# A transformer layer on eight cores: projection weights loaded in eight slices, and the residual load issued by GpSimd

## The chip, the cores and the metric

The kernel runs on all 8 cores of one Trainium2 chip. Each core computes one batch element of eight on its own; the cores exchange nothing. The metric is device time in microseconds of the slowest core. Each core has TensorE (PE, matrix products), VectorE (DVE), ScalarE (ACT), GpSimd (POOL), SyncE (SP) and 16 DMA engines. DMAs are issued here from SP's queue (SPq) and from POOL's queue (POOLq).

## What is computed

One layer of four sub-layers on `x` of shape (8, 2048, 1024), each with its residual. The same `ffn` sub-layer, which is an attention with mixture-of-experts low-rank terms in its projections, is used twice.

```python
x = L0_attn_a_x
x = x + attn_a(layernorm(x), ...)   # causal attention, 16 heads of 64         ("a1")
x = x + ffn(layernorm(x), ...)      # full attention, MoE low-rank projections ("f1")
x = x + attn_b(layernorm(x), ...)   # retention, below                         ("b1")
x = x + ffn(layernorm(x), ...)      # the same as f1                           ("f2")

# attn_b, cut:
q = (x @ Wq.T).reshape(B, L, H, DH)
v = (x @ Wv.T).reshape(B, L, H, DH)
state = _retention_scan(v, jax.nn.sigmoid(beta))
y = (q * state).reshape(B, L, D)
y = (y - mu) * jax.lax.rsqrt(var + LN_EPS) * ln_gamma + ln_beta
y = y * jax.nn.silu(x @ Wg.T)
return y @ Wo.T
```

## The kernel before

Activations are kept transposed: 1024 features in 8 tiles of 128 partitions (`ND = 8`), 2048 positions in 4 chunks of 512 (`NC = 4`, `CH = 512`). `XLN` is the normalised input, `ACT2` the input of an output projection; both are 8 tiles of 128x2048 in bf16. Weights lie in HBM as f32 and are cast to bf16 by the DMA, which for that reason is issued by POOL.

The kernel is a list of stages (`nc.Block`), each with one hand-written program per engine, ordered by semaphores. At the end of a block all engines meet, so no DMA of a stage is issued before the stage before has ended. Seven stages have the same inner form, a product of a 1024x1024 weight with 8 activation tiles:

- **The output projections**, `emit_oproj`, called for a1, f1, b1 and f2. The weight tile is `WOB` (128 x 8x1024, bf16). In a1, f1 and f2 (`do_cn`) the stage first normalises the attention's context: 512 small matmuls on PE and 64 multiplications on DVE. Then, in f1 and f2 (`ffn`), come 32 matmuls for the low-rank term. Then the projection, a loop over `dt2` (0 to 7, output tiles of 128 features), here called a **step**, with four chunks in each. A chunk is 8 accumulating matmuls of 128x128 by 128x512 (L1119), with a ninth in f1 and f2 (L1125), into one of **two** PSUM banks. DVE adds the old residual (`XOLD`) and writes `XNEW` (L1150 or L1155). PE may be two chunks ahead of DVE. SP stores `XNEW` to HBM (L1048); before that it has loaded `XOLD` (L1063), 128x2048 f32, 1 MB. Both tiles have two buffers. In a1, f1 and b1 the next LayerNorm's column sums (8 short matmuls, L152 and L157, for tile `dt2`-2) stand at the head of a step from step 2 on. f2 has none.
- **The Q, V and G projections of `attn_b`**, in `emit_attnb`, blocks `bq`, `bv` and `bg`. The weight tile is `WB`, chunks go into three PSUM banks, 8 matmuls each (L1231, L1309, L1471). In `bv` DVE scans along time after every step.

Before the change each weight comes in two DMAs of 512 columns (1024 KB of bf16 each), counted by the semaphores `gq` and `gqb`. PE waits for the first half ahead of step 0 and for the second ahead of step 4. In the output projection SP's order is: `XOLD` 0, `XOLD` 1, then for each later step: wait until DVE has finished step `dt2`-2, load `XOLD` `dt2`, store `XNEW` `dt2`-2.

The semaphore `to` (`tp`, `tv`, `tg2` in `attn_b`) counts chunks that PE has finished, `vo` chunks that DVE has finished, `oq` the loads of `XOLD`, `so` the stores.

Of the kernel before, what the change touches and what calls it, by code (L numbers as in the profile page):

```python
# [16 lines left out]
ND = 8  # L17
# [5 lines left out]
NC = 4  # L23
# [924 lines left out]
def emit_oproj(P, bufs, tag, wo_name, src_res_name, dst_name, ffn,  # L948
# [3 lines left out]
    src_res = bufs[src_res_name]  # L952
# [8 lines left out]
    with (nc.sbuf_tensor(f"wob{tag}", [128, ND * D], BF16)) as WOB, (  # L961
# [71 lines left out]

        @blk.gpsimd
        def _(g):
            for j, ctr in enumerate((gq, gqb)):
                ctr.inc(g.dma_start(
                    WOB[:].rearrange("p (t o) -> p t o", t=ND)[
                        :, :, j * 512:(j + 1) * 512],
                    bufs[wo_name][:, j * 512:(j + 1) * 512].rearrange(  # L1040
                        "(t p) o -> p t o", p=128)), 16)

        def _store(sync, dt2):
            sync.wait_ge(vo.sem, vo0 + nxvso_holder[0] + NC * (dt2 + 1))
# [5 lines left out]

        @blk.sync
        def _(sync):
            for nm in ("sto0", "sto1"):
                if P.ctr[nm].v > so0[0] + so0[1]:
                    pass
            sync.wait_ge(so[0].sem, so0[0])
            sync.wait_ge(so[1].sem, so0[1])
            for dt2 in range(ND):
                if dt2 >= 2:
                    sync.wait_ge(vo.sem, vo0 + nxvso_holder[0] +  # L1060
                                 NC * (dt2 - 1))
                oq[dt2 % 2].inc(
                    sync.dma_start(XOLD[dt2 % 2][:],  # L1063
                                   src_res[dt2 * 128:(dt2 + 1) * 128, :]), 16)
                if dt2 >= 2:
                    _store(sync, dt2 - 2)
            _store(sync, ND - 2)
            _store(sync, ND - 1)
            sync.wait_ge(so[0].sem, so0[0] + 16 * (ND // 2))
            sync.wait_ge(so[1].sem, so0[1] + 16 * (ND // 2))  # L1070

# [27 lines left out]

        @blk.tensor  # L1100
        def _(t):
            t.wait_ge(gq.sem, gq0 + 16)
            t.wait_ge(vn.sem, vn0 + ncn)
            if ffn:
                t.wait_ge(vo.sem, vo0 + NC)
            ng = 0
            for dt2 in range(ND):
                if dt2 == 4:
                    t.wait_ge(gqb.sem, gqb0 + 16)
                if ln is not None and dt2 >= 2:  # L1110
                    ln.colsums(t, dt2 - 2)
                for ch in range(NC):
                    ng += 1
                    if ng > 2:
                        t.wait_ge(vo.sem, vo0 + nxvso + ng - 2)
                    bank = (ng - 1) % 2
                    last = None
                    for dt in range(ND):
                        last = t.matmul(  # L1119
                            PSB[bank][:],  # L1120
                            WOB[:, dt * D + dt2 * 128:dt * D + (dt2 + 1) * 128],
                            ACT2[dt][:, ch * CH:(ch + 1) * CH],
                            start=(dt == 0), stop=((not ffn) and dt == ND - 1))
                    if ffn:
                        last = t.matmul(  # L1125
                            PSB[bank][:],
                            bufs["UP"]["o"][:, dt2 * 128:(dt2 + 1) * 128],
                            bufs["XVS"]["o"][:, ch * CH:(ch + 1) * CH],
                            start=False, stop=True)
                    to.inc(last)  # L1130
            if ln is not None:
                ln.colsums(t, ND - 2)
                ln.colsums(t, ND - 1)
# [47 lines left out]
def emit_attnb(P, bufs):  # L1181
# [4 lines left out]
    with ExitStack() as es:  # L1186
# [7 lines left out]
        gq0b = gqb.v  # L1194
        with (nc.sbuf_tensor("lamr", [1, 16], F32) as LAMR,
# [2 lines left out]

            @blk.gpsimd
            def _(g):  # L1200
                for j, ctr in enumerate((gq, gqb)):
                    ctr.inc(g.dma_start(
                        WB[:].rearrange("p (t o) -> p t o", t=ND)[
                            :, :, j * 512:(j + 1) * 512],
                        bufs["bWqT"][:, j * 512:(j + 1) * 512].rearrange(
                            "(t p) o -> p t o", p=128)), 16)

            @blk.sync
# [7 lines left out]

            @blk.tensor
            def _(t):
                t.wait_ge(gq.sem, gq0 + 16)
                ng = 0  # L1220
                for dt2 in range(ND):
                    if dt2 == 4:
                        t.wait_ge(gqb.sem, gq0b + 16)
                    for ch in range(NC):
                        ng += 1
                        if ng > 3:
                            t.wait_ge(vp2.sem, vp0 + ng - 3)
                        bank = (ng - 1) % 3
                        last = None
                        for dt in range(ND):  # L1230
                            last = t.matmul(  # L1231
                                PSB[bank][:],
                                WB[:, dt * D + dt2 * 128:dt * D + (dt2 + 1) * 128],
                                XLN[dt][:, ch * CH:(ch + 1) * CH],
                                start=(dt == 0), stop=(dt == ND - 1))
                        tp.inc(last)
# [45 lines left out]
        with (nc.sbuf_tensor("bvt", [128, T], BF16) as VB,  # L1282
              nc.sbuf_tensor("bscn", [128, T], F32) as SCN,
              nc.Block("bv") as blk):

            @blk.gpsimd
            def _(g):
                for j, ctr in enumerate((gq, gqb)):
                    ctr.inc(g.dma_start(
                        WB[:].rearrange("p (t o) -> p t o", t=ND)[  # L1290
                            :, :, j * 512:(j + 1) * 512],
                        bufs["bWvT"][:, j * 512:(j + 1) * 512].rearrange(
                            "(t p) o -> p t o", p=128)), 16)

            @blk.tensor
            def _(t):
                t.wait_ge(gq.sem, gq1 + 16)
                ng = 0
                for dt2 in range(ND):
                    if dt2 == 4:  # L1300
                        t.wait_ge(gqb.sem, gq1b + 16)
                    for ch in range(NC):
                        ng += 1
                        if ng > 3:
                            t.wait_ge(vv.sem, vv0 + (ng - 3) + (ng - 3) // 4 * 2)
                        bank = (ng - 1) % 3
                        last = None
                        for dt in range(ND):
                            last = t.matmul(  # L1309
                                PSB[bank][:],  # L1310
                                WB[:, dt * D + dt2 * 128:dt * D + (dt2 + 1) * 128],
                                XLN[dt][:, ch * CH:(ch + 1) * CH],
                                start=(dt == 0), stop=(dt == ND - 1))
                        tv.inc(last)

            @blk.vector
            def _(v):
                ng = 0
                for dt2 in range(ND):
                    v.wait_ge(vv.sem, vv.v)  # L1320
                    for ch in range(NC):
                        ng += 1
                        v.wait_ge(tv.sem, tv0 + ng)
                        bank = (ng - 1) % 3
                        vv.inc(v.tensor_copy(VB[:, ch * CH:(ch + 1) * CH],
                                             PSB[bank][:]))
                    v.wait_ge(vv.sem, vv.v)
                    vv.inc(v.tensor_tensor_scan(
                        SCN[:], LAMC[:, dt2:dt2 + 1].broadcast_to([128, T]),
                        VB[:], 0.0, ALU.mult, ALU.add))  # L1330
                    v.wait_ge(vv.sem, vv.v)
                    vv.inc(v.tensor_tensor(ACT2[dt2][:], QT[dt2][:], SCN[:],
                                           ALU.mult))
# [109 lines left out]
        with (nc.sbuf_tensor("bgt0", [128, T], BF16) as gt0,  # L1443
# [3 lines left out]

            @blk.gpsimd
            def _(g):
                for j, ctr in enumerate((gq, gqb)):  # L1450
                    ctr.inc(g.dma_start(
                        WB[:].rearrange("p (t o) -> p t o", t=ND)[
                            :, :, j * 512:(j + 1) * 512],
                        bufs["bWgT"][:, j * 512:(j + 1) * 512].rearrange(
                            "(t p) o -> p t o", p=128)), 16)

            @blk.tensor
            def _(t):
                t.wait_ge(gq.sem, gq2 + 16)
                ng = 0  # L1460
                for dt2 in range(ND):
                    if dt2 == 4:
                        t.wait_ge(gqb.sem, gq2b + 16)
                    for ch in range(NC):
                        ng += 1
                        if ng > 3:
# [262 lines left out]
```

## Time and profile before

| | us |
|---|---|
| median of 3 runs | 4083.34 |
| lowest and highest | 4075.66 and 4128.11 |
| the profiled execution | 4081.07 |
| its span on the slowest core (core 1) | 4079.5 |
| PE busy | 3068.7 (75%) |
| ACT busy | 1612.8 (40%) |
| DVE busy | 1317.8 (32%) |
| POOL busy | 71.2 (2%) |

The profile covers one execution, on the slowest core. Its page gives the busy time of the engines and the costliest groups of instructions; the trace behind it can be asked for single instructions, for windows of time, for waits, and for the DMAs with their time from issue to landing. The granted clock is TensorE's, as a share of 2.4 GHz. Names of tiles carry the stage: `wobf` is `WOB` in f1 and f2, `xoa`, `xof`, `xob` are `XOLD`, `xna`, `xnf`, `xnb` are `XNEW`, `bwb` is `WB`, `qsla` and `ksla` are 128-column slices of the Q and K weights in the attention of a1 (cast from f32 as well, 256 KB of bf16). The size beside a DMA is that of what is written.

### The profile page before, as it was taken

The page shows a single profiled execution, that of the slowest core. Times are in us where ns is not written, and L with a number is a line of the kernel's source. Part 1 is how long each engine was busy: PE and PEld are TensorE (multiplying, and loading weights), DVE is VectorE, ACT ScalarE, POOL GpSimd, SP SyncE. Part 2 cuts the span into 40 slices and gives each one's busy share as a digit, 9 for nine tenths or more (in the row PEclk, how much of TensorE's full clock was granted, in tenths as well). Part 3 has the DMA queues.
Part 4 walks back from the last instruction along what each step waited for, and adds up shares of the span by engine and source line. Part 5 has one row for each costly group of instructions (what it writes and reads, how often), then busy time and mean ns, then how long its engine had stood idle before and what let it go on. Part 6 is the DMA issues. An engine that isn't in the chain of part 4 may idle for free. (4 is left out here: it accounts for less than half of the span.)

```text
span 4079.5 us, 40781 instructions; the slowest of 8 cores (4055.3 to 4079.5 us)
## 1 busy us (share of the span) xinstructions
PE 3068.7 (75%) x13815; PEld 1267.1 (31%) x13815; DVE 1317.8 (32%) x1955; ACT 1612.8 (40%) x1600; POOL 71.2 (2%) x88
## 2 busy tenths in 40 slices
PE   2678788787557888888887756457387888888888
PEld 0223333334223333333324222122132333333334
DVE  4333333335452222112115445532622111121134
ACT  2034444452300566666672400134003666666640
POOL 0000000000000000000000000000000000000000
PEclk6887888879769888888889877678588888888889
DMA  2200010002321000000002411016211000000014
GB/s 94 31 6 6 6 11 6 1 1 64 122 42 21 6 6 6 6 6 6 1 1 42 145 21 21 0 26 181 31 21 16 6 6 6 6 6 1 1 42 145
DMA packets 95037, 119.22 MB, mean 29 GB/s; under 512 B 61785, under 2 KB 84458, under 8 KB 85500
## 3 DMA queue, kind: packets, MB, share of 16 engines
q0 software_dynamic: 80192, 37.75, 7.5%
q1 hardware_dynamic: 14652, 78.87, 6.1%
q8 instruction: 124, 2.03, 0.2%
q14 instruction: 69, 0.57, 0.0%
HBM read 120.81 MB, written 33.55 MB: 38 GB/s over the span
## 5 line engine op out<-in xcount | busy, mean ns | idle before, releaser
L794 ACT ACTIVATE ringf<-psd,negcb 128x1024 bf16<-128x1024 f32 x1024 | 1060.0, 1124 | 606.4 <-PE psd L742 605.7
L794 ACT ACTIVATE ringa<-psd,negcb 128x1024 bf16<-128x1024 f32 x320 | 337.4, 1116 | 362.5 <-PE psd L742 331.7
L722 PE MATMUL psb<-ringf,vprf 128*65 128x512 bf16 x1024 | 445.7, 435 | 10.4 <-ACT ringf L794 9.1
L739 PE MATMUL psd<-qpairf,kpairf 64*128 64x512 bf16 x1024 | 421.5, 424 | 28.7 <-ACT ringf L794 6.1
L742 PE MATMUL psd<-qpairf,kpairf 64*128 64x512 bf16 x1024 | 429.9, 432 | 0.0
L726 PE MATMUL psb<-ringf,vprf 128*65 128x512 bf16 x1024 | 422.6, 413 | 0.0
L696 PE MATMUL psb<-c_IDENT,densf 1*128 1x1 f32 x1024 | 171.6, 293 | 172.8 <-DVE act L896 172.8
L739 PEld LDWEIGHTS psd<-qpairf,kpairf 64*128 64x128 bf16 x1024 | 91.7, 95 | 459.3 <-issue 458.1
L696 PEld LDWEIGHTS psb<-c_IDENT,densf 1*128 1x128 f32 x1024 | 168.0, 252 | 190.3 <-issue 190.3
L722 PEld LDWEIGHTS psb<-ringf,vprf 128*65 128x65 bf16 x1024 | 114.2, 112 | 301.4 <-issue 293.7
L772 ACT ACT_TABLE_LOAD x3 | 3.8, 1283 | 495.6 <-DVE grow L847 495.6
L818 DVE TENSOR_SCALAR qpairf<-psb,fbq 128x512 bf16<-128x512 f32 x64 | 48.0, 751 | 372.2 <-PE psb L662 372.2
L722 PE MATMUL psb<-ringa,vpra 128*65 128x512 bf16 x320 | 138.4, 433 | 36.9 <-DVE ringa L873 36.3
L696 PE MATMUL psb<-c_IDENT,densa 1*128 1x1 f32 x512 | 101.0, 322 | 84.3 <-DVE act L896 84.3
L822 DVE TENSOR_SCALAR kpairf<-psb,fbk 128x512 bf16<-128x512 f32 x64 | 48.1, 751 | 342.8 <-PE psb L662 342.8
L656 PE MATMUL psb<-xln,qslf 128*128 128x512 bf16 x512 | 136.9, 416 | 23.1 <-DMA kslf<-fWkT 17.1
L552 PE MATMUL psd<-wvbf,xln 128*128 128x512 bf16 x512 | 128.3, 396 | 27.4 <-DMA wvbf<-fWvT 27.4
L888 DVE COPY densf<-psb 1x512 f32<-1x512 f32 x64 | 43.8, 685 | 301.1 <-PE psb L726 299.0
L1011 PE MATMUL psd<-c_IDENTB,reciph 128*64 128x128 bf16 x768 | 110.5, 225 | 39.8 <-DVE act L1029 29.3
L873 DVE TENSOR_TENSOR ringa<-ringa,c_MASKS 128x1024 bf16<-128x1024 bf16 x128 | 88.6, 692 | 150.6 <-ACT ringa L794 150.6
L739 PE MATMUL psd<-qpaira,kpaira 64*128 64x512 bf16 x320 | 134.5, 440 | 3.1 <-ACT ringa L794 0.9
L656 PE MATMUL psb<-xln,kslf 128*128 128x512 bf16 x512 | 130.2, 400 | 8.1 <-DVE kpairf L822 6.0
(273 smaller groups left out, 4040.7 us busy)
## 6 DMA issues: line engine op xcount, KB each, us to landing
xof<-Xs SPq DMA_DIRECT2D x16, 1024.0 KB, 7.3
lnsta<-xT SPq DMA_DIRECT2D x8, 1024.0 KB, 5.7
xoa<-xT SPq DMA_DIRECT2D x8, 1024.0 KB, 6.7
Xs<-xna SPq DMA_DIRECT2D x8, 1024.0 KB, 8.7
Xs<-xnf SPq DMA_DIRECT2D x8, 1024.0 KB, 10.3
xob<-Xs SPq DMA_DIRECT2D x8, 1024.0 KB, 6.7
Xs<-xnb SPq DMA_DIRECT2D x8, 1024.0 KB, 8.5
y<-xnf SPq DMA_DIRECT2D x8, 1024.0 KB, 8.6
```

Source lines behind the costliest of these rows:

```text
L552: last = t.matmul(PSB[bank][:], XLN[dt][:, m * 128:(m + 1) * 128], WVB[:, dt * 512:(dt + 1) * 512], start=(dt == 0), stop=((not ffn) and d ...
L656: last = t.matmul(PSB[bank][:], sl[p % 2][:, dt * 128:(dt + 1) * 128], XLN[dt][:, ch * CH:(ch + 1) * CH], start=(dt == 0), stop=((not ffn) ...
L696: last = t.matmul(DEN[:, col:col + 1], DENS[0:1, half * 2 * CH + h01 * CH + sub * 128: half * 2 * CH + h01 * CH + (sub + 1) * 128], bufs[" ...
L722: t.matmul(PSB[4][0:65, :], VP[tkpv][:, hA * 65:hA * 65 + 65], RING[slot][:, 0:512], start=(tkpv == 0), stop=(tkpv == n - 1))
L726: last = t.matmul(PSB[5][0:65, :], VP[tkpv][:, hB * 65:hB * 65 + 65], RING[slot][:, 512:1024], start=(tkpv == 0), stop=(tkpv == n - 1))
L739: t.matmul(pd[:, 0:512], KP[p % 2][0:64, ks], QP[p % 2][0:64, cs], start=True, stop=True, tile_position=(0, 0))
L742: ts.inc(t.matmul(pd[:, 512:1024], KP[p % 2][64:128, ks], QP[p % 2][64:128, cs], start=True, stop=True, tile_position=(64, 0)))
L794: ex.inc(s.activation(RING[slot][:], pd[:], AF.Exp, bias=NEGC[:, p:p + 1], scale=softmax_scale))
L818: ins = v.tensor_scalar(dstb[p % 2][:, cs], PSB[7][:], bufs["FBQ"][:, p:p + 1], ASCALE, ALU.add, ALU.mult)
L822: ins = v.tensor_scalar(dstb[p % 2][:, cs], PSB[7][:], bufs["FBK"][:, p:p + 1], None, ALU.add)
L873: vm.inc(v.tensor_mul(RING[slot][:], RING[slot][:], ms))
L1011: last = t.matmul(PSB[bank][0:64, sub * 128:(sub + 1) * 128], rp[:, col:col + 1].broadcast_to([128, 64]), bufs["IDENTB"][:], start=(rp is ...
```

## The change

- Each of the seven weights comes in eight DMAs of 128 columns (one for each step) in place of two of 512, alternately on `gq` and `gqb`. Slices 0 and 1 are issued at the start of the stage; slice j from 2 on is issued after PE has finished step j-2. PE waits for slice `dt2` at the head of step `dt2`.
- In the output projection the load of `XOLD` moves from SP's program to POOL's, between the weight slices. POOL's order is: slices 0 and 1, then for `dt2` from 0 to 7: wait until DVE has finished step `dt2`-2 (from `dt2` = 2), load `XOLD` `dt2`, and, up to `dt2` = 5, wait until PE has finished step `dt2` and load slice `dt2`+2.
- SP's program keeps the stores alone.

What is computed, and from what, stays the same. The core of the diff (the blocks `bv` and `bg` change as `bq` does):

```diff
         @blk.gpsimd
         def _(g):
-            for j, ctr in enumerate((gq, gqb)):
-                ctr.inc(g.dma_start(
+            def wob_dma(j):
+                (gq, gqb)[j % 2].inc(g.dma_start(
                     WOB[:].rearrange("p (t o) -> p t o", t=ND)[
-                        :, :, j * 512:(j + 1) * 512],
-                    bufs[wo_name][:, j * 512:(j + 1) * 512].rearrange(
+                        :, :, j * 128:(j + 1) * 128],
+                    bufs[wo_name][:, j * 128:(j + 1) * 128].rearrange(
                         "(t p) o -> p t o", p=128)), 16)
+
+            off = NC if ffn else 0
+            wob_dma(0)
+            wob_dma(1)
+            for dt2 in range(ND):
+                if dt2 >= 2:
+                    g.wait_ge(vo.sem, vo0 + nxvso_holder[0] + NC * (dt2 - 1))
+                oq[dt2 % 2].inc(
+                    g.dma_start(XOLD[dt2 % 2][:],
+                                src_res[dt2 * 128:(dt2 + 1) * 128, :]), 16)
+                j = dt2 + 2
+                if j < ND:
+                    g.wait_ge(to.sem, to0 + off + (j - 1) * NC)
+                    wob_dma(j)
...
             for dt2 in range(ND):
-                if dt2 >= 2:
-                    sync.wait_ge(vo.sem, vo0 + nxvso_holder[0] +
-                                 NC * (dt2 - 1))
-                oq[dt2 % 2].inc(
-                    sync.dma_start(XOLD[dt2 % 2][:],
-                                   src_res[dt2 * 128:(dt2 + 1) * 128, :]), 16)
-                if dt2 >= 2:
-                    _store(sync, dt2 - 2)
-            _store(sync, ND - 2)
-            _store(sync, ND - 1)
+                _store(sync, dt2)
...
         @blk.tensor
         def _(t):
-            t.wait_ge(gq.sem, gq0 + 16)
             t.wait_ge(vn.sem, vn0 + ncn)
...
             for dt2 in range(ND):
-                if dt2 == 4:
-                    t.wait_ge(gqb.sem, gqb0 + 16)
+                t.wait_ge((gq, gqb)[dt2 % 2].sem,
+                          (gq0, gqb0)[dt2 % 2] + 16 * (dt2 // 2 + 1))
...
             @blk.gpsimd
             def _(g):
-                for j, ctr in enumerate((gq, gqb)):
-                    ctr.inc(g.dma_start(
+                for j in range(ND):
+                    if j >= 2:
+                        g.wait_ge(tp.sem, tp0 + (j - 1) * NC)
+                    (gq, gqb)[j % 2].inc(g.dma_start(
                         WB[:].rearrange("p (t o) -> p t o", t=ND)[
-                            :, :, j * 512:(j + 1) * 512],
-                        bufs["bWqT"][:, j * 512:(j + 1) * 512].rearrange(
+                            :, :, j * 128:(j + 1) * 128],
+                        bufs["bWqT"][:, j * 128:(j + 1) * 128].rearrange(
                             "(t p) o -> p t o", p=128)), 16)
```

## Rows read from the trace of the kernel before

**Rows 1.** The page: its head, and PE's line of the engine table.
```profile
span 4079.5 us, 40781 instructions; the slowest of 8 cores (4055.3 to 4079.5 us)
...
PE 3068.7 (75%) x13815; PEld 1267.1 (31%) x13815; DVE 1317.8 (32%) x1955; ACT 1612.8 (40%) x1600; POOL 71.2 (2%) x88
```

**Rows 2.** Windows: output projections (a1, f1, wait before b1, b1, f2); Q; V; G.
```profile
core 1: us, PE busy (x) PEld busy (x) DVE busy (x) ACT busy (x) POOL busy (x), PEclk, DMA share, GB/s
1002.60:1064.60 62.00, 61.98 (x306) 26.33 (x308) 21.46 (x32) 27.25 (x15) 0.00 (x0) 1.00 0.71 221
2237.40:2307.80 70.40, 69.25 (x340) 29.48 (x342) 23.41 (x32) 27.26 (x15) 0.00 (x0) 1.00 0.62 194
2750.20:2766.00 15.80, 0.00 (x0) 0.00 (x0) 0.00 (x0) 0.00 (x0) 1.75 (x2) 0.55 0.93 210
2766.00:2834.70 68.70, 65.88 (x312) 27.14 (x312) 22.04 (x32) 27.25 (x15) 0.00 (x0) 0.96 0.71 212
4010.50:4073.80 63.30, 62.48 (x288) 28.04 (x288) 23.24 (x32) 0.00 (x0) 0.00 (x0) 1.00 0.69 216
2382.70:2394.00 11.30, 0.00 (x0) 0.00 (x0) 0.00 (x0) 1.50 (x2) 1.75 (x2) 0.50 0.80 107
2394.00:2451.00 57.00, 56.78 (x257) 25.37 (x257) 21.61 (x32) 0.00 (x0) 0.00 (x0) 0.98 0.10 16
2454.60:2465.50 10.90, 0.00 (x0) 0.01 (x1) 0.00 (x0) 0.00 (x0) 1.76 (x2) 0.50 0.82 115
2465.50:2569.00 103.50, 72.27 (x256) 28.23 (x256) 68.01 (x46) 0.00 (x0) 0.00 (x0) 0.79 0.05 8
2679.50:2690.50 11.00, 0.00 (x0) 0.00 (x0) 0.00 (x0) 0.00 (x0) 1.72 (x2) 0.50 0.82 117
2690.50:2748.00 57.50, 56.91 (x256) 25.33 (x256) 8.58 (x7) 20.12 (x33) 0.00 (x0) 0.97 0.09 15
2481.80:2495.00 13.20, 8.76 (x33) 3.49 (x34) 9.39 (x6) 0.00 (x0) 0.00 (x0) 0.87 0.00 1
```

**Rows 3.** Timeline of PE: steps in f1 and b1 (start, duration; in brackets idle before).
```profile
2254.09 1.90 PE L1119 MATMUL psd<-act,wobf 128*128 128x512 bf16 x8
...
2259.21 1.89 PE L1119 MATMUL psd<-act,wobf 128*128 128x512 bf16 x8 [1.06 <-DVE xnf L1150]
...
2264.16 1.90 PE L1119 MATMUL psd<-act,wobf 128*128 128x512 bf16 x8
...
2273.00 1.90 PE L1119 MATMUL psd<-act,wobf 128*128 128x512 bf16 x8
...
2782.22 3.63 PE L1119 MATMUL psd<-act,wobb 128*128 128x512 bf16 x16
2788.63 5.30 PE L1119 MATMUL psd<-act,wobb 128*128 128x512 bf16 x16 [2.78 <-DVE xnb L1155]
...
2794.83 7.08 PE L1119 MATMUL psd<-act,wobb 128*128 128x512 bf16 x32
...
2802.81 7.08 PE L1119 MATMUL psd<-act,wobb 128*128 128x512 bf16 x32
```

**Rows 4.** POOL's issues of 128-column slices; the page's DMAs (KB each, us to landing).
```profile
508.63 0.87 POOL L637 DMA_DIRECT2D qsla<-aWqT  x1 [90.73 <-PE psb L678]
509.49 0.88 POOL L637 DMA_DIRECT2D ksla<-aWkT  x1
...
qsla<-aWqT POOLq DMA_DIRECT2D x8, 256.0 KB, 4.5
ksla<-aWkT POOLq DMA_DIRECT2D x8, 256.0 KB, 5.8
```

**Rows 5.** The tile view of `xof`: landings of its 16 loads from SP's queue.
```profile
L1063 SPq DMA_DIRECT2D xof<-Xs x16: 319/320/423, 2175.8 to 4058.2; - x16
...
DMA to landing us min/median/max: 5.0/7.3/10.6
```

**Rows 6.** SP's timeline in f2, and the chain that ended last (start, duration).
```profile
4050.48 0.32 SPq L1063 DMA_DIRECT2D xof<-Xs  x1
...
4050.95 9.83 DMA y<-xnf
...
4061.84 1.89 PE psd L1119 x8
```

More of the change, by code:

```diff
@@ L1052, in _ @@
         def _(sync):
-            for nm in ("sto0", "sto1"):
-                if P.ctr[nm].v > so0[0] + so0[1]:
-                    pass
             sync.wait_ge(so[0].sem, so0[0])
@@ L1218, in _ @@
             def _(t):
-                t.wait_ge(gq.sem, gq0 + 16)
                 ng = 0
                 for dt2 in range(ND):
-                    if dt2 == 4:
-                        t.wait_ge(gqb.sem, gq0b + 16)
+                    t.wait_ge((gq, gqb)[dt2 % 2].sem,
+                              (gq0, gq0b)[dt2 % 2] + 16 * (dt2 // 2 + 1))
                     for ch in range(NC):
@@ L1287, in _ @@
             def _(g):
-                for j, ctr in enumerate((gq, gqb)):
-                    ctr.inc(g.dma_start(
+                for j in range(ND):
+                    if j >= 2:
+                        g.wait_ge(tv.sem, tv0 + (j - 1) * NC)
+                    (gq, gqb)[j % 2].inc(g.dma_start(
                         WB[:].rearrange("p (t o) -> p t o", t=ND)[
-                            :, :, j * 512:(j + 1) * 512],
-                        bufs["bWvT"][:, j * 512:(j + 1) * 512].rearrange(
+                            :, :, j * 128:(j + 1) * 128],
+                        bufs["bWvT"][:, j * 128:(j + 1) * 128].rearrange(
                             "(t p) o -> p t o", p=128)), 16)
@@ L1296, in _ @@
             def _(t):
-                t.wait_ge(gq.sem, gq1 + 16)
                 ng = 0
                 for dt2 in range(ND):
-                    if dt2 == 4:
-                        t.wait_ge(gqb.sem, gq1b + 16)
+                    t.wait_ge((gq, gqb)[dt2 % 2].sem,
+                              (gq1, gq1b)[dt2 % 2] + 16 * (dt2 // 2 + 1))
                     for ch in range(NC):
@@ L1449, in _ @@
             def _(g):
-                for j, ctr in enumerate((gq, gqb)):
-                    ctr.inc(g.dma_start(
+                for j in range(ND):
+                    if j >= 2:
+                        g.wait_ge(tg2.sem, tg20 + (j - 1) * NC)
+                    (gq, gqb)[j % 2].inc(g.dma_start(
                         WB[:].rearrange("p (t o) -> p t o", t=ND)[
-                            :, :, j * 512:(j + 1) * 512],
-                        bufs["bWgT"][:, j * 512:(j + 1) * 512].rearrange(
+                            :, :, j * 128:(j + 1) * 128],
+                        bufs["bWgT"][:, j * 128:(j + 1) * 128].rearrange(
                             "(t p) o -> p t o", p=128)), 16)
@@ L1458, in _ @@
             def _(t):
-                t.wait_ge(gq.sem, gq2 + 16)
                 ng = 0
                 for dt2 in range(ND):
-                    if dt2 == 4:
-                        t.wait_ge(gqb.sem, gq2b + 16)
+                    t.wait_ge((gq, gqb)[dt2 % 2].sem,
+                              (gq2, gq2b)[dt2 % 2] + 16 * (dt2 // 2 + 1))
                     for ch in range(NC):
```

## The prediction

> **What bounds the kernel now.** I read the page's head and engine table first: TensorE (PE) is busy 3068.7 us of a 4079.5 us span, and the eight cores lie within 24 us of each other, so one core can be argued from [rows 1]. Then the seven stages that the change touches, in the windows view [rows 2]. In the four output projections PE is busy 61.98 of 62.00 us, 69.25 of 70.40, 65.88 of 68.70 and 62.48 of 63.30, at a granted clock of 0.96 to 1.00. The loads and stores beside them (DMA share 0.62 to 0.71) are hidden there. Loads are not hidden ahead of four stages: 11.30, 10.90 and 11.00 us before the Q, V and G projections, 15.80 us before the b1 output projection, each with PE busy for 0.00.
>
> The PE rows give the length of a step (one `dt2`: four chunks of 512 columns). In b1 it is 7.98 us (2794.83 to 2802.81) [rows 3]: 32 matmuls of 7.0 us and 1.0 us for the LayerNorm sums. The a1 stage is 2x7.0+6x7.98 = 61.9, which is its window. f1 has one matmul more in each chunk: 8.84 us (2264.16 to 2273.00) [rows 3]. f2 has that too but no sums: 63.30/8 = 7.9 us [rows 2].
>
> **The change, part by part.** *Q, V and G projections.* Before, PE starts 11.3, 10.9 and 11.0 us after POOL's first issue [rows 2]. The first slice of 128 columns has the form of the attention's loads `qsla`, which land 4.5 us after issue [rows 4]. With 0.15 to wake PE that is 4.7, three times: **-19.1 us**. Later slices are issued when PE ends step j-2 and are needed when it ends step j-1. One step is 57.0/8 = 7.1 us in Q, 7.2 in G, 103.5/8 = 12.9 in V [rows 2]. 4.7 is less, so those cost nothing; the step hides them with 2.4 us to spare. If a slice took as long as one behind another (0.87+5.8 = 6.7 us [rows 4]), it would still be hidden. Without that cover each of the six later slices of Q and G would cost its whole 4.7 us, 56 us in all.
>
> *Output projections: weight slices.* In a1, f1 and f2 the context is normalised first and the loads lie under that, so an earlier first slice brings nothing. In b1 it does. PE starts at 4.7 us, at the low clock, and is through two chunks at 9.9. `XOLD` 0, third in POOL's queue, is issued at 1.8 and lands at 1.8+5.0+2.2 = 9.0 (the fastest `xof` landing [rows 5], behind one more slice), so that PE's step 0 ends near 13.6. Before, steps 0 and 1 ended at 2781.2 by the row at 2782.22 less the sums [rows 3], so step 0 ended 7.0 earlier, 24.1 us after 2750.2. **-10.5 us.**
>
> *Output projections: the residual load moves to POOL's queue.* This decides. Before, SP issues `XOLD` k when VectorE (DVE) has finished step k-2, a whole step ahead. After, POOL goes in order: `XOLD` k-1, wait until PE has **finished** step k-1, weight slice k+1, `XOLD` k. So the load of step k starts when PE is already entering step k, for k = 1 to 6. (`XOLD` 7 follows right behind `XOLD` 6, since no slice is left to wait for; step 0's load lies under the normalisation, or in b1's sum.) PE can run two chunks ahead of DVE, for there are two banks; then it waits for DVE's first chunk, and DVE waits for `XOLD`. From PE's end of step k-1 to that landing:
> - wake POOL 0.1, issue the slice 0.87 [rows 4];
> - `xof`'s landing after issue, median 7.3 (5.0 to 10.6), most of them with the previous tile's store issued 0.5 us behind [rows 5, 6]; in the changed order the store stands beside it too;
> - the slice ahead of it in the same queue: the second of two slices lands 0.87+5.8-4.5 = 2.2 us after the first [rows 4].
>
> Sum L = 10.5 us. From a landing (4050.95+9.83 = 4060.78) over DVE's chunk to PE's next matmul (4061.84) it is 1.05 us [rows 6]. Then PE does the two chunks left, and slowly: after 2.78 us idle in b1 they took 2794.83-2788.63 = 6.2 with the sums, 5.2 without, against 3.5 at full clock; after 1.06 us idle in f1 a chunk took its normal 1.89 [rows 3]. V's stage, idle 4.4 us of each step, has a granted clock of 0.79 over all and 0.87 in one step, between the levels 1.2 and 2.4 GHz, where Q and G have 0.98 and 0.97 [rows 2]. Here the idle time is L+1.05 less 4.9 us (two chunks and the sums), some 6.6 us, so I charge the slow form: 5.25 us in a1 and b1, 5.6 in f1 and f2 (two matmuls more). A changed step is 10.5+1.05+5.25 = 16.8 us, or 17.15.
>
> The Trainium skill has a rule on the 2.2 us. "DMA: Bandwidth & Descriptors", section "Issuing engines are not separate DMA queues", says that transfers interleave on the same 16 engines whoever issued them and that a second issuer saves only issue time. The section "Queues, rings and completion order" of the same page adds that an engine takes turns between rows and keeps order within one. By the first alone the move of the load costs nothing of its own; by the second it stands behind the slice. The trace has no plain 1 MB load on POOL's queue, so both remain (rival 3).
>
> Steps 1 to 6, six of them, before and after:
> - a1: 7.0+5x7.98 = 46.9; 6x16.8 = 100.8: **+53.9**
> - f1: 7.9+10.07 (its step with the stall, 2254.09 to 2264.16)+4x8.84 = 53.3; 6x17.15 = 102.9: **+49.6**
> - b1: 7.0+12.61 (2782.22 to 2794.83)+4x7.98 = 51.5; 100.8: +49.3, with the -10.5 **+38.8**
> - f2: 6x7.9 = 47.4; 102.9: **+55.5**
>
> Sum +197.8-19.1 = **+178.7 us**. The profiled execution took 4081.07 us (its span 4079.5), 2.3 below the median of 4083.34. 4081.07+178.7 = **4260 us**.
>
> *Bounds.* 1 us of L is 24 us of time. L is bounded by SP's rows: below 0.1+0.87+5.0 = 6.0 us, with nothing for the slice, 4260-24x4.5 = 4152 us; if PE's clock also stays up (24x1.75 less) 4110. Above, 0.1+0.87+10.6+2.2 = 13.8 us, 4339. Nothing lies below that, since no row has this load landing within 5.0 us of its issue. SP only stores now, and 0.5 us sooner; I cost that at nothing, for the waits for stores behind the stalls of b1 and f2 vanish in longer steps (some 5 us, counted above in the old steps).
>
> **The rivals.**
> 1. *The move to POOL is covered* (not slower). If `XOLD` landed within PE's two chunks, only the gains remain: 4081-19.1-10.5 = 4051 us, -0.7%. It needs L+1.05 under 4.9 us, L under 3.8; the fastest landing alone is 5.0. Chance 3%.
> 2. *Short stall.* The load lands at its fastest and PE's clock hardly falls: 4110 to 4150 us. For it: some `xof` did land in 5.0. Against: the median is 7.3, and the slice comes ahead. Chance 7%.
> 3. *The queue costs nothing* (the page's first rule as a mechanism: load and slice share the engines). L = 8.3, 4260-24x2.2 = 4207 us. Against it: two slices on POOL's queue land 2.2 us apart and not together [rows 4]. Chance 20%.
> 4. *PE stays at the low clock for all of both chunks left.* 24x1.75 = 42 us more, 4302 us. b1's row speaks against: 1.7 us over, not 3.5. Chance 10%.
> 5. *A 1 MB load issued by POOL is slower than any of SP's rows,* or the store goes wholly ahead of it: beyond 4339. Chance 5%.
>
> **How the numbers follow.** The forecast holds 55%: 4260 us. The range reaches from the lower bound of L with the slow clock to its upper bound, **4150 to 4340 us**; it takes in rivals 3 and 4 and leaves out the other three, under 2 in 10. Under 2% (82 us) is about what a measurement of this kernel can't tell from no change. Slower by over 2% are the forecast and rivals 3, 4 and 5, **0.90**. Within 2% are rivals 1 and 2 but for a bit, **0.08**. Faster by over 2% has no mechanism, since all waits ahead of the four stages sum to 49 us: **0.02**.
>
> **What would show it.** The windows of the output projections at 115 to 120 us, with PE's clock under 0.95. DVE waiting for the DMA of `xo` at the first chunk of steps 1 to 6, 24 waits; PE in turn waiting for DVE 24 times, some 6.6 us each. `xo` landing about 9.5 us after its issue. PE starting in Q, V and G 4.7 us after POOL's first issue and never waiting for `bwb` later. The forecast is wrong if `xo` lands within 4 us, if the steps hold at 8 us, or if PE waits for weight slices in the middle of Q or G.

## The result and the profile after

The changed kernel is slower: the ratio to the kernel before is 1.0492 (95% interval 1.0454 to 1.053). The forecast was slower, 4260 us within 4150 to 4340; nine runs gave a median of 4300.12 us, the lowest 4268.19, and the profiled execution took 4270.47 us with a span of 4268.9. Some executions of any of these kernels, those before too, run at a lower TensorE clock on one die or both and take some per cent longer; spans, landings and stage times below come from cores at the ordinary clock.

The page of the changed kernel, PE's line and the DMA queues (packets, MB, share of 16 engines):

```profile
PE 3118.2 (73%) x13815; PEld 1277.4 (30%) x13815; DVE 1318.6 (31%) x1955; ACT 1612.6 (38%) x1600; POOL 126.3 (3%) x162
...
q0 software_dynamic: 128480, 71.31, 10.2%
q1 hardware_dynamic: 10044, 45.31, 3.4%
```

PE did the same 13815 matmuls in 49.5 us more of busy time [rows 1], so most of the 189.4 us between the two spans (core 1 before, core 2 after, each the slowest of its kernel) is idle time. The windows view of the changed kernel, in the order of [rows 2] (the four output projections, b1 with its wait in front; then wait and projection of Q, V and G):

```profile
1005.10:1125.20 120.10, 74.39 (x310) 28.75 (x312) 21.21 (x32) 27.25 (x15) 9.20 (x13) 0.82 0.49 136
2296.60:2419.00 122.40, 82.05 (x344) 31.82 (x344) 23.48 (x32) 27.70 (x16) 9.18 (x13) 0.82 0.47 133
2841.80:2968.30 126.50, 78.06 (x310) 29.38 (x312) 21.24 (x32) 27.25 (x15) 11.49 (x16) 0.80 0.52 141
4143.00:4264.00 121.00, 74.93 (x288) 30.36 (x288) 23.48 (x32) 0.00 (x0) 9.18 (x13) 0.82 0.48 135
2492.00:2496.60 4.60, 0.00 (x0) 0.01 (x1) 0.00 (x0) 1.50 (x2) 1.76 (x2) 0.50 0.95 87
2496.60:2554.80 58.20, 58.09 (x257) 25.69 (x257) 21.52 (x32) 0.00 (x0) 5.27 (x6) 0.95 0.31 30
2558.50:2562.90 4.40, 0.00 (x1) 0.03 (x1) 0.00 (x0) 0.00 (x0) 1.75 (x2) 0.66 0.95 93
2562.90:2668.00 105.10, 73.26 (x256) 28.40 (x256) 68.53 (x47) 0.00 (x0) 5.26 (x6) 0.77 0.17 16
2777.80:2782.30 4.50, 0.04 (x1) 0.07 (x2) 0.00 (x0) 0.00 (x0) 1.75 (x2) 0.50 0.94 93
2782.30:2839.80 57.50, 56.80 (x256) 25.21 (x256) 8.58 (x7) 20.31 (x33) 5.26 (x6) 0.97 0.31 30
```

The waits ahead of Q, V and G fell from 11.3, 10.9 and 11.0 to 4.6, 4.4 and 4.5 us. The output projections went from 62 to 70 us to 120 to 122 us, at a granted clock of 0.80 to 0.82 in place of 0.96 to 1.00 [rows 2]. By the tile views, which give the start of the first and last matmul of a stage (for b1 and for Q, V, G from POOL's first issue to the last matmul), in us:

| stage | before | after | change |
|---|---|---|---|
| a1 output projection | 61.5 | 119.2 | +57.7 |
| f1 | 69.4 | 120.4 | +51.0 |
| b1, from the issue | 83.3 | 125.6 | +42.3 |
| f2 | 62.6 | 119.4 | +56.8 |
| Q, V, G, from the issue | 67.7, 113.7, 67.6 | 62.2, 108.2, 60.9 | -17.7 |
| sum | | | +190.1 |

The sum is the difference of the two spans, 189.4 us, within a microsecond. It compares two different cores. Over all eight cores these stages grew by 195.0 us on average and the spans by 187.8, so some 7 us came back elsewhere. Core 1 also waits longer than any other core of the kernel before: 11.3 us ahead of Q, where the others wait 8.6 to 10.6. On average over the cores, Q, V and G gained 15.3 us, not 17.7.

Who waits for whom, over the whole changed kernel (us, times, longest):

```profile
PE psd L1120 <- DVE xnf L1151: 84.9, 12, 8.0
...
PE psd L1120 <- DVE xna L1156: 45.6, 6, 8.5
PE psd L1120 <- DVE xnb L1156: 43.9, 7, 8.4
```
```profile
DVE xnf L1151 <- DMA xof<-Xs: 115.8, 12, 10.2
...
DVE xnb L1156 <- DMA xob<-Xs: 69.6, 7, 11.3
...
DVE xna L1156 <- DMA xoa<-xT: 61.9, 6, 11.4
```

25 waits of DVE for the residual load, 247.3 us, and behind them 25 waits of PE for DVE, 174.4 us. PE's idle time in the four windows is 45.7+40.4+48.4+46.1 = 180.6 us, so these waits are nearly all of it, and they stand in the six steps of each stage that the forecast named (the 25th is b1's step 0). One such step in a1, from the timelines of PE and POOL:

```profile
1041.52 5.01 PE L1120 MATMUL psd<-act,woba 128*128 128x512 bf16 x16 [7.91 <-DVE xna L1156]
1047.43 3.63 PE L1120 MATMUL psd<-act,woba 128*128 128x512 bf16 x16
1057.93 5.33 PE L1120 MATMUL psd<-act,woba 128*128 128x512 bf16 x16 [6.88 <-DVE xna L1156]
```
```profile
1047.08 0.89 POOL L1037 DMA_DIRECT2D woba<-aWoT  x1 [16.01 <-PE psd L1120]
1047.95 0.56 POOL L1050 DMA_DIRECT2D xoa<-xT  x1
```

PE ends a step at 1046.53 (1041.52+5.01). POOL notices at 1047.08, issues the slice, then the load; it lands 8.8 us later, at 1056.8, and PE goes on at 1057.93. Two chunks at full clock show as 3.63 us, the two after the stall as 5.01 and 5.33.

### The profile page after: what moved, and what is told of

Its sections match the earlier page's. It is cut to its first block and busy times, and to the rows that moved or that the text cites. A ratio compares the mean times of both kernels' runs of the same rounds, so it can differ in the third digit from the quotient of the medians.

```text
span 4268.9 us, 40907 instructions; the slowest of 8 cores (4245.4 to 4268.9 us)
## 1 busy us (share of the span) xinstructions
PE 3118.2 (73%) x13815; PEld 1277.4 (30%) x13815; DVE 1318.6 (31%) x1955; ACT 1612.6 (38%) x1600; POOL 126.3 (3%) x162
## 3 DMA queue, kind: packets, MB, share of 16 engines
q0 software_dynamic: 128480, 71.31, 10.2%
q1 hardware_dynamic: 10044, 45.31, 3.4%
## 5 line engine op out<-in xcount | busy, mean ns | idle before, releaser
L722 PE MATMUL psb<-ringf,vprf 128*65 128x512 bf16 x1024 | 445.3, 435 | 10.5 <-ACT ringf L794 9.1
L1120 PE MATMUL psd<-act,wobf 128*128 128x512 bf16 x512 | 142.7, 429 | 87.0 <-DVE xnf L1151 84.9
L739 PE MATMUL psd<-qpaira,kpaira 64*128 64x512 bf16 x320 | 134.7, 441 | 3.0 <-ACT ringa L794 0.9
L742 PE MATMUL psd<-qpaira,kpaira 64*128 64x512 bf16 x320 | 135.8, 444 | 0.0
```

The lines of the kernel that those rows point to most:

```text
L722: t.matmul(PSB[4][0:65, :], VP[tkpv][:, hA * 65:hA * 65 + 65], RING[slot][:, 0:512], start=(tkpv == 0), stop=(tkpv == n - 1))
L739: t.matmul(pd[:, 0:512], KP[p % 2][0:64, ks], QP[p % 2][0:64, cs], start=True, stop=True, tile_position=(0, 0))
L742: ts.inc(t.matmul(pd[:, 512:1024], KP[p % 2][64:128, ks], QP[p % 2][64:128, cs], start=True, stop=True, tile_position=(64, 0)))
L1120: last = t.matmul(PSB[bank][:], WOB[:, dt * D + dt2 * 128:dt * D + (dt2 + 1) * 128], ACT2[dt][:, ch * CH:(ch + 1) * CH], start=(dt == 0), ...
```

## The experiments

**The residual loads back on SP, the slices kept.**

```diff
         @blk.gpsimd
...
-                oq[dt2 % 2].inc(
-                    g.dma_start(XOLD[dt2 % 2][:],
-                                src_res[dt2 * 128:(dt2 + 1) * 128, :]), 16)
...
         @blk.sync
...
-                _store(sync, dt2)
+                if dt2 >= 2:
+                    sync.wait_ge(vo.sem, vo0 + nxvso_holder[0] +
+                                 NC * (dt2 - 1))
+                oq[dt2 % 2].inc(
+                    sync.dma_start(XOLD[dt2 % 2][:],
+                                   src_res[dt2 * 128:(dt2 + 1) * 128, :]), 16)
+                if dt2 >= 2:
+                    _store(sync, dt2 - 2)
```

> The changed kernel with the residual loads back in SP's program, as before the change; all weights still in eight slices. My theory (the late issue of the residual load makes the whole loss, the slices themselves are a gain): the output projections are back at 62 to 70 us each, Q, V and G still start 4.6 us after POOL's first issue, so the time is 4081 - 19 - 10 = about 4050 us, ratio 0.993. Rival (slices of 128 columns, issued step by step, cost on PE's path): PE waits for weight slices in the steps, time at or above 4081 us.

Measured: ratio 1.0141 (1.0072 to 1.0209), lowest 4129.43 us, a span of 4127.9. That is 0.7 to 2.1% slower than the kernel before: neither the 4050 us of my theory nor the loss of the changed kernel. The a1 stage took 83.2 us (61.5 before, 119.2 in the changed kernel). DVE no longer waits for any `xo` load; PE waits for weight slices. The tile view of this kernel, and its waits of PE:

```profile
L1037 POOL DMA_DIRECT2D wobf<-fWoT x16: 873/873/881, 2193.8 to 4095.1; - x16
...
DMA to landing us min/median/max: 9.1/11.4/16.3
```
```profile
PE psd L152 <- DMA wobb<-bWoT: 19.5, 3, 11.4
PE psd L1122 <- DMA wobf<-fWoT: 19.4, 3, 9.3
...
PE psd L152 <- DMA woba<-aWoT: 16.1, 3, 5.5
PE psd L1122 <- DMA wobb<-bWoT: 11.6, 1, 11.6
...
PE psd L152 <- DMA wobf<-fWoT: 9.6, 2, 5.6
```

A slice that lands in 4.0 to 4.8 us (medians) in this kernel's Q, V and G stages takes 11.4 us beside a load and a store of 1 MB on SP's queue, and it has one step of 7 to 9 us to come in. So the slices are a second cause of loss, which the changed kernel hides behind the first: the rival was right on this point.

**POOL's loads one step earlier.**

```diff
...
+            xo_dma(0)
+            xo_dma(1)
+            for dt2 in range(ND - 2):
+                g.wait_ge(to.sem, to0 + off + (dt2 + 1) * NC)
+                wob_dma(dt2 + 2)
+                g.wait_ge(vo.sem, vo0 + nxvso_holder[0] + NC * (dt2 + 1))
+                xo_dma(dt2 + 2)
...
```

> The changed kernel with the residual loads still on POOL's queue, but XOLD k issued when DVE has finished step k-2, a step earlier than in the change, behind slice k. Theory (what costs is the moment of the issue): like the kernel before, less the gains, 4050 to 4065 us, a load's landing near 9 us but under the step. Rival (a 1 MB load on POOL's queue is slow wherever it stands): steps of more than 10 us, time above 4130 us.

Measured on one execution: 4071.24 us (span 4069.7), the a1 stage 70.6 us. PE's line in the tile view of `woba`, and the only wait inside the projections of PE for a DVE that adds the residual:

```profile
L1121 PE MATMUL psd<-act,woba x256: 376/379/634, 1005.0 to 1075.6; 128*128 128x512 bf16 x128
```
```profile
PE psd L1121 <- DVE xnf L1152: 0.6, 1, 0.6
```

The loads land in 9.2 us in f1 and f2 and 11.9 in a1, slower than in the changed kernel, and PE hardly waits for them: what costs is the moment of the issue, not the landing. It missed 4050 to 4065 us by 6. Here too PE waits for slices inside the steps, 7.3 us in a1, 7.9 in f1 and f2, 8.2 in b1.

**The load ahead of the slice at the same moment.**

```diff
...
+            for dt2 in range(1, ND):
+                if dt2 < ND - 1:
+                    g.wait_ge(to.sem, to0 + off + dt2 * NC)
+                if dt2 >= 2:
+                    g.wait_ge(vo.sem, vo0 + nxvso_holder[0] + NC * (dt2 - 1))
+                xo_dma(dt2)
+                if dt2 + 1 < ND:
+                    wob_dma(dt2 + 1)
...
```

> The changed kernel with XOLD k issued ahead of weight slice k+1, both at the same late moment as in the change (PE has finished step k-1). Theory of a queue in order: the load is issued 0.9 us earlier and has no slice ahead of it (2.2 us), so each of 24 steps is 3.1 us shorter: 4269 - 74 = about 4195 us. Rival (the load and the slice share the engines, the order in the queue costs nothing): only the 0.9 us of issue, 4269 - 21 = about 4248 us.

Measured on one execution: 4223.64 us, span 4222.1, so 46.8 us off, 1.95 a step. The landing of `xof` fell from a median of 8.9 to 7.9 us. The step gains 0.87 of issue and 1.0 in the queue. That lies midway between the two theories: the slice ahead in the queue costs something, but 1.0 us and not the 2.2 charged.

**The late loads issued by SP.**

The slices alone stay on POOL, as in the run sp_loads; SP's part of the edit:

```diff
...
             for dt2 in range(ND):
-                _store(sync, dt2)
+                if 1 <= dt2 < ND - 1:
+                    sync.wait_ge(to.sem, to0 + off + dt2 * NC)
+                oq[dt2 % 2].inc(
+                    sync.dma_start(XOLD[dt2 % 2][:],
+                                   src_res[dt2 * 128:(dt2 + 1) * 128, :]), 16)
+                if dt2 >= 1:
+                    _store(sync, dt2 - 1)
+            _store(sync, ND - 1)
...
```

> The changed kernel with XOLD k issued by SP, at the same late moment as in the change (PE has finished step k-1), the slices alone on POOL. Theory: the stall stays, since it comes from the moment and not from the queue; landing about 7.3 us after an issue that comes 0.9 us earlier, so a wait of 7.5 in place of 9.9 us, 24 x 2.4 = 58 us off, about 4210 us. Rival (POOL's queue is the cause): back to 4050 to 4080 us.

> The kernel of the run sp_late once more, since that one ran at a TensorE clock of 0.76 on all cores, which its comparison kernels did not. From its steps of 12.5 to 15 us (17.0 to 17.4 in the changed kernel): 24 x 3.4 = 80 us off the changed kernel, about 4190 us. If the queue were the cause of the loss: 4050 to 4080 us.

Measured: the first run took 4352.37 us at a clock of 0.76 to 0.77 on all cores, and that time is not used. The repeat gave 4184.15 us with a span of 4182.6; `xof` landed in 6.6 us, the a1 stage took 96.3 us. One step in a1, from the timelines of PE, SP and POOL:

```profile
1028.29 6.02 PE L1121 MATMUL psd<-act,woba 128*128 128x512 bf16 x16 [5.45 <-DVE xna L1157]
```
```profile
1034.38 0.33 SPq L1067 DMA_DIRECT2D xoa<-xT  x1
```
```profile
1034.85 0.87 POOL L1037 DMA_DIRECT2D woba<-aWoT  x1 [15.12 <-PE psd L1121]
```

PE ends the step at 1034.31. SP and POOL wait for the same semaphore: SP issues 0.07 us later, POOL 0.54 later. So issuing the load from SP is worth 86.3 us of the changed kernel's loss, 3.6 a step. The rows account for it: 0.5 us of waking, 0.9 of the slice's issue ahead of the load, and 2.3 of landing (8.9 to 6.6), 3.7 in sum. The other 103 us of loss remain with the load on SP's queue, where PE waits 90.6 us for DVE behind the late loads and only 2.9 for slices inside the steps, so they come from the late moment. Moving the load to POOL is not the main cause; issuing it from POOL at that moment makes it worse.

**The kernel before, with its loads moved to POOL.**

```diff
         @blk.gpsimd
...
+            for dt2 in range(ND):
+                if dt2 >= 2:
+                    g.wait_ge(vo.sem, vo0 + nxvso_holder[0] + NC * (dt2 - 1))
+                oq[dt2 % 2].inc(
+                    g.dma_start(XOLD[dt2 % 2][:],
+                                src_res[dt2 * 128:(dt2 + 1) * 128, :]), 16)
...
         @blk.sync
...
             for dt2 in range(ND):
-                if dt2 >= 2:
-                    sync.wait_ge(vo.sem, vo0 + nxvso_holder[0] +
-                                 NC * (dt2 - 1))
...
+                _store(sync, dt2)
```

> The kernel before (weights in two halves at the start of the stage), with only the residual load moved from SP's to POOL's queue; POOL waits for nothing there but DVE's step k-2, as SP did. Theory (the moment costs, not the queue): within 10 us of the kernel before, 4081 us, but in b1, where XOLD 0 stands behind the whole weight, some 5 us more. Rival (a 1 MB load on POOL's queue is slow in itself): DVE waits for XOLD in most steps, time above 4120 us.

Measured: 4073.5 us, span 4072.0; the a1 stage 61.6 us. From the page of the kernel before (first line) and from this kernel's:

```profile
Xs<-xna SPq DMA_DIRECT2D x8, 1024.0 KB, 8.7
```
```profile
xof<-Xs POOLq DMA_DIRECT2D x16, 1024.0 KB, 7.9
...
Xs<-xna SPq DMA_DIRECT2D x8, 1024.0 KB, 5.1
```

DVE waited for no `xof`; it waited 2.9 us for `xoa`, once, and 21.1 for `xob`, twice. The queue does change the landings: the loads take longer (6.7 to 7.3 us before, 7.9 to 9.1 here), the stores on SP's queue are faster (8.5 to 10.3 before, 4.4 to 5.2 here), and so are the halves of the weight in a1, f1 and f2 (17.2 to 19.0, and 10.2 to 10.8). But with a step of lead, nearly all of it is covered. The four output projections took 268.4 us on average over the eight cores, 272.5 before, and b1 did not lose the 5 us expected (77.1, before 78.0). At this moment the queue by itself costs nothing.

**PE kept busy through the stall.**

```diff
...
+                    if ch == 2 and 1 <= dt2 < ND - 1:
+                        for _ in range(30):
+                            t.matmul(PSB[4][:],
+                                     WOB[:, dt2 * 128:(dt2 + 1) * 128],
+                                     ACT2[0][:, 0:CH], start=True, stop=True)
...
```

> The changed kernel with 30 extra matmuls of 512 columns (6.5 us at full clock, result not used, into a bank that the stage leaves free) between the second and third chunk of steps 1 to 6 of every output projection, where PE otherwise stands idle for 7 to 8 us. The stall's end is set by the landing of XOLD, so the extra work lies under it. Theory (the two chunks after the stall run at the low clock and cost 1.5 to 1.9 us each step): 24 x 1.7 = 41 us off the changed kernel's 4269, about 4228 us, and the granted clock of the output projections near 1. Rival (the stall is the wait alone, the clock costs nothing there): 4269 us or more.

The same step in a1, from PE's timeline of this kernel (L1117 are the extra matmuls):

```profile
1031.62 3.63 PE L1125 MATMUL psd<-act,woba 128*128 128x512 bf16 x16
1035.08 6.64 PE L1117 MATMUL psb<-act,woba 128*128 128x512 bf16 x30
1042.42 3.61 PE L1125 MATMUL psd<-act,woba 128*128 128x512 bf16 x16 [0.70 <-DVE xna L1161]
```

The granted clock of the two chunks after the stall (PEclk, the third value from the right), in the changed kernel and in this one:

```profile
1041.50:1046.50 5.00, 4.98 (x18) 1.83 (x20) 1.16 (x2) 0.00 (x0) 0.00 (x0) 0.71 0.00 0
```
```profile
1042.40:1046.00 3.60, 3.58 (x18) 1.51 (x20) 1.16 (x2) 0.00 (x0) 0.00 (x0) 1.00 0.00 0
```

They take 3.61 us again at a clock of 1.00, in place of 5.01 at 0.71: the slow form is the clock's, and it goes when PE does not stand idle. The clock of the four projections is 0.95 to 1.00 here, as expected, and 0.80 to 0.82 in the changed kernel. The stages gave a1 107.8, f1 114.6, f2 114.4 us (119.2, 120.4, 119.4), but b1 127.0 from the issue (125.6). The span is 4250.4, 18.5 us off, not 41. b1 is an outlier of this core: the other seven took 116.6 to 120.1 us, against 123.2 to 127.0 in the changed kernel. Over all eight cores the four projections fell by 25.5 us on average. The rest of the 41 was given back: the residual loads landed later here, a median of 9.4 in a1, 9.6 in f and 10.3 in b1 against 9.0, 8.9 and 8.9. Why, the runs don't show.

**The stores cut.**

```diff
-    src_res = bufs[src_res_name]
+    src_res = bufs["xT"]
...
+            w = 16 if ln is not None else T
             so[dt2 % 2].inc(
-                sync.dma_start(dst[dt2 * 128:(dt2 + 1) * 128, :],
-                               XNEW[dt2 % 2][:]), 16)
+                sync.dma_start(dst[dt2 * 128:(dt2 + 1) * 128, 0:w],
+                               XNEW[dt2 % 2][:, 0:w]), 16)
```

> The changed kernel with the stores of a1, f1 and b1 cut to 16 of 2048 columns and every stage's residual read from the kernel's input, so that its result is not the reference's; f2 stores in full. It takes the store's share out of the wait for XOLD. Theory (the store, on SP's queue, is served beside the slice and the load, and delays both): in a1, f1 and b1 the slice lands after 4.5 us instead of 7.2 and XOLD after 6.5 instead of 8.9, so 18 steps are 2.4 us shorter, about 4225 us, and f2 keeps its 17.4 us steps. Rival (the landing of 8.9 us is POOL's own): no step shorter, 4269 us.

This kernel leaves out most of what a1, f1 and b1 should store and adds the kernel's input as every residual; it serves the measurement alone. The lowest time was 4302.22 us, with cores 4 to 7 at a clock of 0.79 to 0.80, so the comparison is by cores 0 to 3 (die 0): a median span of 4214.8 us against 4259.0 for the same cores of the changed kernel, 44.2 off, as expected. On core 1, the slices `wobf` in the window of f1 (stores cut) and then in that of f2 (stores whole), then `xof` in the same two:

```profile
DMA to landing us min/median/max: 4.0/4.5/7.1
...
DMA to landing us min/median/max: 4.3/7.5/7.7
```
```profile
DMA to landing us min/median/max: 6.1/6.7/8.7
...
DMA to landing us min/median/max: 8.3/9.1/11.0
```

Within one kernel, the store of 1 MB beside them costs the slice 3.0 us and the load 2.4. Steps of f1 are 14.3 to 16.1 us apart, those of f2 still 17.1 to 18.0.

**Slices two steps ahead, loads on SP.** The edit against the run sp_loads:

```diff
...
-            for j in range(2, ND):
-                g.wait_ge(to.sem, to0 + off + (j - 1) * NC)
+            wob_dma(2)
+            for j in range(3, ND):
+                g.wait_ge(to.sem, to0 + off + (j - 2) * NC)
...
```

> The kernel of the run sp_loads, with weight slice j of the output projections issued when PE has finished step j-3 instead of j-2 (three slices at the start of the stage), each slice with a semaphore of its own. In sp_loads the slices landed 11.4 us after issue beside SP's loads and stores and PE waited for them. Theory (the margin of one step is too short for a slice that has to share the engines with 2 MB a step, and two steps are enough): no waits for slices in steps 2 to 7, the output projections of a1, f1 and f2 at 61 to 71 us, about 4055 us. Rival (slices in steps cost by their own traffic, however early): still above 4081 us.

Measured: the lowest run took 4078.01 us, the longest span of die 0 was 4077.4 (core 2). The waits for slices inside the steps fell from 65 us in the run sp_loads (76 with the 11.6 us ahead of b1's step 0) to 4.3, as expected, and the a1 stage from 83.2 to 69.0. The time did not come down to 4055: DVE now waits for the stores of `XNEW`, 16.2, 21.5 and 10.7 us for a1, for f1 with f2, and for b1 (2.5, 12.8 and 5.7 in the kernel before), and the stores land in 9.8 to 10.5 us (8.5 to 10.3). This fits the rival in part: slices in the steps seem to slow the stores beside them, however early they are issued. It rests on one execution without an interval, and its span is hardly below the 4079.5 of the kernel before.

**Only Q, V and G.** Against the kernel before:

```diff
 def emit_attnb(P, bufs):
...
-                for j, ctr in enumerate((gq, gqb)):
+                for j in range(ND):
+                    if j >= 2:
+                        g.wait_ge(tp.sem, tp0 + (j - 1) * NC)
...
```

> Only the Q, V and G part of the change (eight paced slices); the output projections as in the kernel before. By the stages of the changed kernel, 5.5 + 5.5 + 6.8 = 18 us less than the kernel before, ratio 0.9956, about 4063 us. Rival (a part of the 18 us is given back later): within 5 us of the kernel before.

The output projections are those of the kernel before. Measured: ratio 0.9965 (0.9948 to 0.9982), lowest 4060.9 us. This part of the change is a gain, of 0.2 to 0.5%.

**A version from the findings.** Two places of the edit, against the kernel before:

```diff
...
+                for j in range(ND):
+                    wb_dma(g, j, "bWqT")
+                for j in range(ND):
+                    g.wait_ge(tp.sem, tp0 + (j + 1) * NC)
+                    wb_dma(g, j, "bWvT")
...
+            n, sems = (2, (gq, gqb)) if do_cn else (ND, W)
...
```

> A version after the findings so far. Output projections of a1, f1 and f2 as in the kernel before. In b1 all eight slices are issued at the start, with no wait for PE, and SP issues XOLD 0 only when slice 0 has landed. Q, V and G in slices; the slices of V are loaded into the same tile during Q, each as soon as PE has used the old one, and those of G during V. Each slice has a semaphore of its own. Theory: Q gains 6.6 us, V and G their whole 11 us each, b1 about 8 us of its 15.8: 4081 - 37 = about 4045 us, ratio 0.991. Rival (slices behind SP's loads and stores in b1 land late): b1 gains nothing or loses, 4052 to 4065 us.

Measured: ratio 0.9931 (0.9914 to 0.9948), median 4060.41 us, lowest 4052.89. It beats both kernels, by about 28 us against the kernel before; 37 were expected. V and G gained about what they should: from Q's last matmul to V's first it is 5.9 us (15.1 before), from V's last to G's first 110.9 (122.3). Two terms fell short. Q starts 8.1 us after POOL's first issue on this core (core 5) and not 4.6. The eight slices on the queue at once are not enough to explain it, since cores 1, 3, 4, 6 and 7 issue the same eight and start after 4.4 to 5.1; why three cores start later stays open. And b1 took 81.1 us from the issue in place of 83.3 (76.5 and 78.0 on average over the cores), since `XOLD` 0, issued only after slice 0 had landed, kept DVE waiting 15.7 us: there the rival was right that b1 gains almost nothing.

## Why the prediction was right, and where its terms were off

**The step that decided** held. The load of step k went out when PE had ended step k-1, and the steps became 17.01 us in a1, 16.92 in b1, 17.38 in f1 and 17.40 in f2 (the mean of five intervals between POOL's slice issues), where 16.8 and 17.15 were forecast. The run with loads one step earlier was 199 us faster and so took all of the loss back, the same late moment on SP's queue kept 103 us of it, and the queue alone did nothing. What stands behind the waits is the order of two waits in one instruction stream.

**The sum L was right, its terms were not.** Forecast 0.1+0.87+7.3+2.2 = 10.5 us; measured 0.55+0.87+8.9 = 10.3. That the sum fits so well is luck: two errors of opposite sign cancel. POOL's waking takes 0.55 and not 0.1 us (1046.53 to 1047.08, and so in four of the five steps 1 to 5 of a1). No row of the prediction gave the 0.1; it is what SP takes (0.07 to 0.10 us in the run sp_late2). The slice ahead costs 1.0 and not 2.2 us, as the run with the order swapped shows, and the load with nothing ahead lands in 7.9, not 7.3. I had taken the 2.2 from two slices with nothing beside them [rows 4]; here the store is in flight as well, and it costs the load 2.4 us (small_store), more than the slice does.

**The rule on the queues.** The changed kernel has the plain load on POOL's queue that the trace of before lacked. The Trainium skill, "DMA: Bandwidth & Descriptors", "Issuing engines are not separate DMA queues", says that DMAs run on the same 16 engines and interleave whoever started them, and that issuing from several engines saves only issue time. In the total this case agrees where the loads have a step of lead: the kernel before and the same kernel with its loads on POOL's queue lie within 8 us. At the late moment it does not: the stall was 86 us longer in sum with POOL's queue than with SP's, and the slice's issue is 24x0.87 = 21 us of that. Another 11 us (24x0.47) is POOL's later waking, and some 55 (24x2.3) is the landing, which the sentence on issue time does not cover. "Queues, rings and completion order" on the same page, by which an engine takes turns between rows packet by packet, fits what the landings show: with the load moved off SP's queue and nothing else changed, the stores left there land in 4.4 to 5.2 us instead of 8.5 to 10.3 (the run before_pool), and a slice with two SP transfers beside it takes 11.4 us. The mean packet is 71.31 MB/128480 = 555 B on POOL's queue and 45.31 MB/10044 = 4.5 KB on SP's. That turns are taken so was not tested by itself.

**The clock** was rightly charged: 5.0 to 5.4 us for two chunks in a1's steps 1 to 5 (5.25 forecast), with 6.9 to 8.0 us of idle time before them. `warm` gives 1.4 to 1.8 us of it back in each of these steps, where 1.75 was forecast; in the whole time only 18.5 us came out.

**Sizes.** +190.1 against +178.7 us. The steps being 0.2 us longer is 5 us. a1's step 6 is another 2.4: its PE idle time is 8.52 us and its two chunks take 6.41, while `XOLD` 6 and 7 are both on the queue. Q and V took 1 us or more each between first and last matmul than before; the forecast had -19.1 for the three, they gave -17.7. b1's step 0 ended 13.8 us after the issue (13.6 forecast). Two to three us are not assigned. The gains were read from core 1, whose waits ahead of Q, V, G and b1 are the longest of the eight. On the other cores there was less to gain; one core does not stand for all here.

**A step that was wrong and did not show.** "Later slices cost nothing" was argued for Q, V and G, where it holds (PE never waits for `bwb` after the first slice). Rival 1 then took it for the output projections too: 4051 us if the load were covered. With the load covered the runs gave 4071 and 4129 us, because slices issued one step ahead land too late beside 2 MB a step. I had read the landing of a slice from a stage without other traffic. The 4051 us was too low, and the rival's time should have been worked out with a slice's landing in the traffic of that stage.

## What to carry to other kernels

In a queue with waits written out in order, a transfer is issued no earlier than the latest wait ahead of it. Before putting a prefetch behind another stream's wait, write down which step each load is issued in and which step needs it: here the move cost one step of lead, and with it 17 us steps for 8 us steps. A gain from splitting a load (a first slice in 4.5 us in place of 11) is worth having where PE stands waiting at the start of a stage; for slices issued in mid-stage, take the landing from rows with the same traffic beside them, not from a quiet stage.

## What the runs showed of the hardware

- The same 128-column slice on POOL's queue lands in 3.9 to 4.8 us (medians) in Q, V and G, 7.1 to 7.5 beside a 1 MB store on SP's queue and ahead of a 1 MB load on its own, and 10.9 to 11.4 beside a 1 MB load and store on SP's. The load on SP's queue is not slowed by the slice: `xof` 7.1 us in that last case, against 7.3 before [rows 5].
- With the load on POOL's queue in place of SP's and all else the same, the 1 MB stores on SP's queue land in 4.4 to 5.2 us in place of 8.5 to 10.3, and the loads in 7.9 to 9.1 in place of 6.7 to 7.3 (the run before_pool).
- POOL starts its DMA 0.55 us after PE's last matmul of the step has ended by the profile, in four of the five steps 1 to 5 of a1 (0.9 in the other). SP, waiting for the same semaphore, starts 0.07 to 0.10 us after it (the run sp_late2, four steps).
- After PE stood idle for 6.9 to 8.5 us, the next 16 matmuls took 5.0 to 6.4 us instead of 3.6 (a1 of the changed kernel; 0.71 of the clock in the step shown). With 30 matmuls put into the stall (0.7 to 1.7 us idle left) they took 3.61 at 1.00, though these do no useful work.
